# Tail of a fused adaLN block: output weights multiplied once by the last batch's gate, and one rank step placed behind another projection

## The reference

```python
mod = (_silu(c) @ wmod).reshape(B, 6, 1, -1)
sa, ca, ga, sb, cb, gb = (mod[:, k] for k in range(6))   # per batch; |ga|, |gb| held at 0.25 or more
h = _layernorm(x) * (1 + ca) + sa
x = x + ga * attention(h)            # softmax over the query axis, causal; z @ W_o.T + b_o
h = _layernorm(x) * (1 + cb) + sb
x = x + gb * ffn(h)                  # top-1 of 16 experts, at most 256 tokens each, others dropped
```

## Time and profile before

| | |
|---|---|
| median of 3 runs | 1314.1 us (1311.01 to 1314.48) |
| profiled execution | 1314.31 us, its span 1312.6 us, granted clock 0.959 |
| PE busy | 1207.0 us, 92% of the span |
| DVE, ACT, POOL busy | 857.4, 600.9, 342.4 us |

### The profile page before, as it was taken

One profiled execution on the slowest core, in us unless ns is written; L12 is line 12 of the kernel. 1 busy time (PEld: TensorE's weight loads), 2 busy tenths in 40 slices (PEclk: granted clock), 3 DMA queues, 4 the chain that ended last, 5 costly groups with the idle time before them and its releaser, 6 DMA issues.

```text
span 1312.6 us, 23573 instructions
## 1 busy us (share of the span) xinstructions
PE 1207.0 (92%) x7518; PEld 856.0 (65%) x7518; DVE 857.4 (65%) x2159; ACT 600.9 (46%) x1419; POOL 342.4 (26%) x529
## 2 busy tenths in 40 slices
PE   5788888888999999999999999999998939999995
PEld 2555555555666666666666666666665739999994
DVE  6566666656767676666776666676665555767673
ACT  2455555555555555555555555554554013232320
POOL 3221212212232323232332212233433340111111
PEclk7899999988999999999999999999999968999998
DMA  4521202001222222221212212134435744676630
GB/s 149 191 80 60 105 24 105 31 34 57 77 69 64 72 66 86 68 74 57 72 56 70 80 57 72 58 101 140 155 120 193 257 153 147 223 237 217 235 125 18
DMA packets 100243, 139.66 MB, mean 106 GB/s; under 512 B 9916, under 2 KB 71486, under 8 KB 100032
## 3 DMA queue, kind: packets, MB, share of 16 engines
q1 hardware_dynamic: 91600, 113.55, 26.2%
q10 hardware_dynamic: 4464, 16.25, 3.1%
q0 software_dynamic: 4096, 8.82, 1.8%
HBM read 94.50 MB, written 48.00 MB: 109 GB/s over the span
## 4 chain that ended last, share of the span: by engine, by line
PE 73%; issue 11%; ACT 7%; DVE 6%; POOL 2%; DMA 1%; DVEq 0%; ACTq 0%; SPq 0%; POOLq 0%
PE SC L799 18%; PE Z L819 15%; PE Z L973 9%; PE SC L946 7%; ACT E L1014 7%; PE XA L855 6%; PE XA L771 5%; PE XA L781 4%; PE XB L781 3%; PE XB L771 2%; PE SC L735 1%; PE XB L841 1%; DVE V L1303 1%; DVE nm L1315 1%; DVE SC L1315 1%
## 5 line engine op out<-in xcount | busy, mean ns | idle before, releaser
L1014 ACT ACTIVATE E<-SC,nm 128x512 f32<-128x512 f32 (+7 forms) x512 | 375.0, 740 | 422.4 <-DVE nm L1315 422.4
L1315 DVE CUSTOM_DVE_ANT_0 SC<-SC,mask 128x512 f32<-128x512 f32 (+7 forms) x512 | 376.1, 786 | 220.0 <-PE SC L799 220.0
L799 PE MATMUL SC<-XQ,XK 64*128 64x512 f32 (+3 forms) x2304 | 271.3, 368 | 50.7 <-ACT E L1014 48.4
L799 PEld LDWEIGHTS SC<-XQ,XK 64*128 64x128 f32 x2304 | 188.8, 192 | 150.9 <-issue 133.9
L819 PE MATMUL Z<-E,vs 128*64 128x512 f32 (+3 forms) x1536 | 270.6, 494 | 0.3 <-DVE vs L1291 0.3
L819 PEld LDWEIGHTS Z<-E,vs 128*64 128x64 f32 x1536 | 100.0, 137 | 137.2 <-issue 127.3
L973 PE MATMUL Z<-W,hh 128*128 128x256 f32 x512 | 114.8, 383 | 2.3 <-issue 2.3
L973 PEld LDWEIGHTS Z<-W,hh 128*128 128x128 f32 x512 | 97.2, 192 | 15.5 <-issue 2.7
L1014 ACT ACTIVATION_READ_ACCUMULATOR E<-SC,nm 128x1 f32 x512 | 101.4, 198 | 0.0
L855 PE MATMUL XA<-woT,zt 128*128 128x256 f32 x384 | 89.3, 385 | 0.0
L1105 ACT ACTIVATE hh<-SC,b1t 128x256 f32<-128x256 f32 x64 | 26.9, 471 | 121.3 <-PE SC L946 121.3
(11 more groups left out here) (247 smaller groups left out, 2001.3 us busy)
## 6 DMA issues: line engine op xcount, KB each, us to landing
W<-in_w SPq DMA_DIRECT2D x32, 1024.0 KB, 8.1
z_s<-zs ACTq DMA_DIRECT2D x31, 512.0 KB, 2.6
zt<-z_s SPq DMA_DIRECT2D x24, 512.0 KB, 3.8
W<-in_wqk SPq DMA_DIRECT2D x33, 257.0 KB, 2.7
slots_s<-zt SPq DMA_DIRECT2D x16, 520.0 KB, 3.9
xb<-slots_s SPq DMA_DIRECT2D x16, 520.0 KB, 3.8
Wv<-in_wv SPq DMA_DIRECT2D x17, 256.0 KB, 2.6
xln<-in_x SPq DMA_DIRECT2D x24, 128.0 KB, 2.4
```

Of the source, the lines that this page charges most:

```text
L799: last = pe.matmul(SC[h][:, at:at + z - a], XK[rows, ap, kp, lo:lo + P], XQ[rows, ap, qp, a:z], start=(t == 0), stop=(t == 2))
L1014: act.activation(E[:, h, EOFF[kb]:EOFF[kb + 1]], SC[h][:, at:at + S - lo], ACT.Exp, bias=nm[:, h, kb:kb + 1], scale=-1.0, accum_out=rs[:, ...
L1315: dve.tensor_tensor_reduce(SC[h][:, at:at + S - lo], SC[h][:, at:at + S - lo], mask[:, 0:S - lo], 1.0, BIG, ALU.add, ALU.min, nm[:, h, kb: ...
```

## The change

DVE multiplies `woT` by the last batch's gate row, in two instructions of 128x1024, into a new tensor `woG`. It lies on the first half of `XQ`, whose pair is done by then. The two stand in the last attention step, behind `scale_values(1)` and behind `reduce(5)`. `project_out` multiplies with `woG`, and waits for both; `norm_tail` loses L1438 and adds the bank straight to the tokens' rows. On PE `lot_ranks(1, XA)` moves from ahead of `project_out(2)` to behind it. On POOL `tail_pow(2)` moves ahead of `lot_scatter(0)`, and `tail_pow(3)` ahead of `lot_scatter(1)`. Eight semaphores of the second lot's scatters become one, `lot_scattered`.

```diff
+        gated, below = ExitStack(), top[0]
+        sb("left_below_q", [P, (place["XQ"] - top[0]) // 4], stack=gated)
+        woG = sb("woG", [P, PAIRS, D], stack=gated)
+        assert place["woG"] == place["XQ"]
+        gated.close()
...
-        tp = zt[:, 0, 2 * NC:4 * NC, :].rearrange("p (q c) t -> p q (c t)", q=2)
...
-            for k in range(HS):
-                sp.wait_ge(scattered[k], 16)
+            sp.wait_ge(lot_scattered, 16 * HS)
...
                 pe.wait_ge(tail_z, 32)
+                pe.wait_ge(wo_gated, 2)
...
-                        last = pe.matmul(bank, z[:, u * P:(u + 1) * P], woT[:, c, :], start=(c == 0), stop=(c == PAIRS - 1))
+                        last = pe.matmul(bank, z[:, u * P:(u + 1) * P], woG[:, c, :], start=(c == 0), stop=(c == PAIRS - 1))
...
             project_out(1)
             turn(0)
+            project_out(2)
             pe.wait_ge(auxa_free, TOTAL["auxa"])
             pe.wait_ge(auxb_free, TOTAL["auxb"])
             lot_ranks(1, XA)
-            project_out(2)
             gate(0)
...
+            def gate_weights(half):
+
+                cs = slice(half * PAIRS // 2, (half + 1) * PAIRS // 2)
+                dve.tensor_tensor(woG[:, cs, :], woT[:, cs, :], modB[:, B - 1, GA, :].unsqueeze(1).broadcast_to([P, PAIRS // 2, D]),
+                                  ALU.mult).then_inc(wo_gated, 1)
...
                 if att:
                     scale_values(1)
+                    if not proj:
+                        gate_weights(0)
                     reduce(4)
                     reduce(5)
+                    if not proj:
+                        gate_weights(1)
...
-                follow(dve.tensor_tensor(part, bank.rearrange("p (q d) -> p q d", q=size), each(modB[:, B - 1, GA, :]), ALU.mult))
                 dve.wait_ge(tail_xg, n + 1)
-                follow(dve.tensor_tensor(x1_, part, x1_, ALU.add))
+                follow(dve.tensor_tensor(x1_, bank.rearrange("p (q d) -> p q d", q=size), x1_, ALU.add))
...
             tail_pow(1)
+            tail_pow(2)
             lot_scatter(0)
-            tail_pow(2)
+            tail_pow(3)
             lot_scatter(1)
-            tail_pow(3)
```

More of the change, by code:

```diff
@@ L353, in adaln_block @@
         W1 = sb("W1", [P, 2, NC, HID])
+        gated, below = ExitStack(), top[0]
[3 more added lines that the diff above has]
+        gated.close()
+        top[0] = below
         W1h = sb("W1h", [P, 2, NC, HID], F32R)
@@ L472, in adaln_block @@
         tail_x = sem("tail_x")
+        wo_gated = sem("wo_gated")
         tail_wo = sem("tail_wo")
@@ L489, in adaln_block @@
         ext_ok = sem("ext_ok")
-        scattered = [sem(f"scattered{k}") for k in range(HS)]
+        lot_scattered = sem("lot_scattered")
         we_in = [sem(f"we_in{k}") for k in range(NW)]
@@ L1433, in each @@
                     return row.unsqueeze(1).broadcast_to([P, size, D])
-                x1_, h2_, part = th[:, tiles, D:2 * D], th[:, tiles, 0:D], tp[:, 0:size, :]
+                x1_, h2_ = th[:, tiles, D:2 * D], th[:, tiles, 0:D]
                 bank = SC[u0 // 4][:, u0 % 4 * D:(u0 % 4 + size) * D]
                 dve.wait_ge(tail_wo, n + 1)
-                follow(dve.tensor_tensor(part, bank.rearrange("p (q d) -> p q d", q=size), each(modB[:, B - 1, GA, :]), ALU.mult))
                 dve.wait_ge(tail_xg, n + 1)
-                follow(dve.tensor_tensor(x1_, part, x1_, ALU.add))
+                follow(dve.tensor_tensor(x1_, bank.rearrange("p (q d) -> p q d", q=size), x1_, ALU.add))
                 for q in range(size):
@@ L1778, in lot_scatter @@
                     pool.indirect_dma_start(slots_s, bass.IndirectOffsetOnAxis(slot_u[:, t:t + 1], 0), hs[:, k, :], None,
-                                            bounds_check=NE * CAP - 1, oob_is_err=False).then_inc(scattered[k], 16)
+                                            bounds_check=NE * CAP - 1, oob_is_err=False).then_inc(lot_scattered, 16)
             def tail_scatter(n):
```

## The result

| | median (lowest to highest), us | profiled execution: own time, span, clock |
|---|---|---|
| before | 1312.49 (1310.54 to 1315.42), 20 runs | 1314.31, 1312.6, 0.959 |
| after | 1309.39 (1308.25 to 1311.94), 20 runs | 1309.30, 1307.5, 0.968 |

The ratio is 0.9976, with a 95% interval of 0.9969 to 0.9982: 3.1 us faster (2.4 to 4.1), or 0.24%. That is on the "no change" side of the 0.3% that I had set, but the sign is sure. Four runs of three of the experiments' kernels further down (ranks_only, weights_only, scatter_5_3) took 2,006 to 5,542 us; they are in the medians of those kernels and in none of the ratios.

What follows compares the result with a forecast made beforehand. Only the tail and the last attention step could move, through the chain of PE, DVE's norms and POOL's roots. Gain 1.8 less 0.35 lost, 1.45, say 1.5 us, off 1314.1 gives 1312.6 us; range 1309.8 to 1315.4.

Steps and rivals of the forecast that it cites:

- PE's order: PE in the tail: `project_out(2)` follows `turn(0)` at once, ranks done at 1044.1, last pair delivered 2.3 us earlier.
- DVE's new wait: DVE in the tail: `lot_take(1)` waits 2.4 us for the ranks; `norm_tail(2)` starts at 1046.3, 1.1 earlier.
- The norm's cut: DVE in the tail: each `norm_tail` loses L1438, 0.72 us of 6.20, leaving 5.48.
- POOL's order: POOL in the tail: `tail_pow(3)` waits 1.2 us for `lot_scatter(0)`; the last norm ends 1.8 us earlier, not 3.0.
- the surplus: POOL's scatter between the last two roots: one issue takes 1.56 us against a median of 0.97; 0.59 kept as repeating.
- the waits don't bite: Rival, 17%: POOL's issue isn't held and DVE keeps its turn in the last step; 2.3 to 2.4 us gained, 1311.7.
- The last step: Last attention step: the first weights' multiply meets POOL's adds, taking some 2.2 us instead of 1.22; 0.35 us lost.
- The base: Starting time of the forecast: 1314.1 us, the median of before, from which 1.5 was subtracted.
- the clock's rival: Rival, 18% either way: PE's switch to 2.4 GHz at the experts' start shifts, moving the result 1.5 us: 1314.1 or 1311.1.
- One of my own signs of being wrong: Whole span: the forecast is wrong if the span's end moves by other than the experts' first transposes do.

Runs made afterwards that it cites:

- ranks_only: The kernel before with only the second lot's ranks moved behind `project_out(2)` on PE; ratio 1.0005, median 1313.72 us.
- weights_only: The changed kernel with PE's and POOL's order of before, so only the weights' multiply and shorter norms; ratio 0.9990, median 1311.39 us.
- scatter_5_3: The changed kernel with five of the second lot's eight scatters ahead of the last root, three behind, instead of four and four; ratio 0.9990, median 1312.47 us.
- after_again: The changed kernel, unchanged, profiled and timed once more on another chip; ratio 0.9977 against the kernel before, median 1309.33 us.
- before_again: The kernel before, unchanged, profiled and timed once more on another chip; ratio 1.0000, median 1312.67 us.
- scatter_3_5: The changed kernel with three of the second lot's eight scatters ahead of the last root, five behind; ratio 0.9971, median 1309.07 us.
- early_and_3_5: The changed kernel with both weights' multiplies ahead of `reduce(1)` and scatters split three and five; ratio 0.9965, median 1308.62 us.
- best_try: The changed kernel, weights' multiplies early, ranks between `project_out(2)`'s tiles, `project_out(3)` right behind, first logits in the last root's wait; ratio 0.9969, median 1308.74 us.

## Why the prediction was right or wrong

**PE's order: right.** `project_out(2)` follows `turn(0)` without a gap, and DVE takes up the ranks at 1044.10, forecast 1044.1.

**DVE's new wait: right.** 2.33 us, forecast 2.4; `norm_tail(2)` starts at 1046.31, forecast 1046.3; the last pair is taken up at 1052.30, forecast 1052.3.

**The norm's cut: right for the later norms, unfinished for the first.** weights_only shows 1.58 us of gain in a tail where I had then looked for 0 to 0.6; about 1 of it comes by way of the first norm and PE's gap. In the whole change the ranks stand behind that gap, so the sum didn't suffer.

**POOL's order: the step that failed.** "This alignment repeats by construction when `lot_scatter(0)` follows `tail_pow(2)`, so I keep the 0.59." It doesn't. The last root started 34.49 us behind `project_out(0)`, where 37.12 had been: 2.63 earlier, and I had 1.86. Of the missing 0.77, 0.64 lie between the last two roots (6.58 us where 7.22 had been), and 0.49 of these are the held issue (1.07 for 1.56). I had put the surplus at 0.59, against the median of 0.97; but the first issue of a scatter takes 1.07 even where no such DVE instruction is beside it (in before, the one at 1045.52), so the surplus was 0.49 from the start. The other 0.13 is `norm_tail(2)`, which asks for its root a little sooner than worked out. The rival "the waits don't bite" had 2.4 for the tail's end, and 2.5 was measured (40.20 to 37.66 us from `project_out(0)` to the end of the last norm). Its other half, no loss in the step, did not hold in the first pair of traces.

**The last step: right mechanism, too small.** I had 0.35, with 0.7 as the upper bound. The multiply took 2.30, forecast 2.2; PE waited 0.49 for the exponentials; the step grew by 0.60 in five of the six traces that have the multiply beside the adds. In after_again it didn't (28.46 against 28.44): its multiply is held as well (2.29), but the scaling ahead of it took 0.46 instead of 1.23, and PE, slower by the clock, reached the scores of these maxima no sooner; they start at 1009.99, and at 1010.02 in before_again. By these traces the term is 0.6 or nothing, and it was nothing where the clock had fallen ahead of it.

**The base: the largest part.** I subtracted from 1314.1, the median of three runs. With 20 runs it is 1312.5, 1.6 lower; in the 82 runs of the kernel before that the experiments are set against the times go from 1310.5 to 1315.2. I wrote that the three runs lay 3.5 us apart, and put this to the clock's rival, but not to the base. This is half of the miss of 3.2 us. The tail is 0.9 more (2.68 for 1.8), with the held issue in it; the step takes 0.25 back (0.60 for 0.35); about 1 is left, of which the next paragraph speaks.

**The clock's rival: a part of it, and what stays open.** By step and tail of the first pair of traces the change should give 2.68 - 0.60 = 2.1 us, and 3.1 and 3.0 were measured, with 2.4 and 1.7 as the lower ends. Both pairs show what can fill this: where the experts start, PE is back at 2.4 GHz sooner behind the first transposes in the kernel after (0.92 and 0.30 us), and in the second pair the step isn't lengthened. That second pair adds up to 3.0 with nothing left over. So that rival, which had 1311.1 for the case of a gain, named the right place. How much it gives on the mean of all runs isn't shown: there are two traces of each kernel. One of my own signs of being wrong is there as well: in the first pair the span's end moved by 5.1 us and the first transposes by 2.6.

The mean clock of the runs doesn't settle it: of the 82 runs of before 29 have a mean clock of 0.961 or less and a median of 1313.6, the others 1312.45; of the 29 runs of after and after_again seven have, with 1310.85 against 1309.3. Within either kind the distance is about 3, but a mean over the whole span doesn't tell where the clock was low.

## What to carry to other kernels

When one engine's stall is filled, ask at once which queue its result goes to next: here PE's filled gap was worth nothing until two roots of 0.7 us had changed places with chains of 5 us on POOL. Put the short instruction that others wait for ahead of the long chain that nobody waits for. Before a forecast in tenths of a per cent, ask how far the median of so few runs can lie off; here that was half of the error.

## What the runs showed of the hardware

**A few hundredths of a us decide whether a scatter's issue is held.** In before_again, POOL and DVE:

```profile
1052.05 1.56 POOL L1778 DMA_INDIRECT slots_s<-xb,slot_u  x1 [0.81 <-POOL xb L1774]
```

```profile
1052.00 0.69 DVE L1450 TENSOR_TENSOR th<-th,modB 128x512 f32<-128x512 f32 x1
```

Six traces show an issue of 1.55 to 1.59, each starting 0.05 to 0.06 behind the start of a DVE instruction with two SBUF inputs (before, before_again, scatter_5_3, scatter_3_5, early_and_3_5, best_try); in ranks_only one starts 0.23 behind and takes 1.41. Where the distance was 0.03 to 0.04 (17 issues in twelve of the fourteen traces, two in each of after and after_again), the issue took 1.05 to 1.07, which is what it takes with nothing beside it (1.07 in before at 1045.52), and DVE's instruction 0.76 or 0.77 instead of 0.69. So one of the two waits, DVE for 0.07 us or POOL for 0.5. It isn't chance of the single run: before and before_again show the held issue both, after and after_again don't. But the order of the program alone doesn't settle it. In scatter_5_3 the copy ahead of the same issue as in after covers five tiles instead of four and takes 224 ns instead of 217; the issue starts 49 ns behind DVE's instruction instead of 41, and is held, 1.59 for 1.07. The Trainium skill ("SBUF — State Buffer", Who interferes with whom) infers that a scatter's descriptor writing isn't held by such a DVE instruction. Here issues are held, by 0.5 us; but an indirect one also takes its slot numbers from SBUF (`slot_u`), and no run separates the two, so the inference isn't refuted. That the two engines meet on the port which the page describes is its explanation, and no run here shows it.

**The clock adds its own spread.** Ahead of the last expert's 32 matmuls PE stands idle for 2.28 us in both kernels. Behind it the clock was at 1.2 GHz for a part in three of the fourteen traces (before 8.76 us, weights_only 8.79, scatter_5_3 8.78), and at 2.4 GHz throughout in the others (7.16). This one event is 1.6 us, half of what the change brings, and it falls one way or the other in the same kernel. With the 0.76 in the last attention step, the clock alone moves one trace of a kernel against another by as much as the parts of this change. The Trainium skill ("TensorE: Matmul & The Clock Gate", Part 1) says that the moment of the switch varies with where the work lands in a window that runs on its own; the two profiles of before agree, 8.76 against 7.16, and no row shows the window.
